# A tuned attention + two-MoE kernel: the constants tile moved by 192 bytes in SBUF

## The reference, cut to what matters

```
x1  = x + attention(rmsnorm(x, norm1_scale), Wq, bq, ..., Wo, bo)      # 16 heads of 16, chunks of 64
...
# first MoE: xf = rmsnorm(x1); top 2 of 8 experts, capacity 1280 rows each
h   = gelu(xf[tok] @ W1[eid] + b1[eid]) @ W2[eid] + b2[eid]            # 256 -> 1024 -> 256
out = out.at[tok].add(gate[:, None] * h)
...
x   = layernorm(x + x1 + out)
# second MoE: xn = layernorm(x) * gamma + beta; top 2 of 8, capacity 1280
g, u = split(xb @ w12.T);  h = silu(g) * u;  yb = h @ w3.T             # 256 -> 2 x 1024 -> 256
x   = layernorm(x + out2)
```

## Time and profile before

| | us |
|---|---|
| median of three executions | 1483.54 |
| lowest of them | 1483.48 |
| profiled execution, its own time | 1478.57 |
| its span, first to last instruction | 1476.8 |

### The profile page before, as it was taken

How to read it: one execution, slowest core, us unless ns; L and a number is a source line. 1 busy time by engine, 2 the same in 40 slices (tenths; PEclk the granted TensorE clock), 3 DMA queues, 4 the chain that set the end, 5 groups by cost and what they waited for, 6 DMA issues and landing times. The chain is left out here.

```text
span 1476.8 us, 36143 instructions
## 1 busy us (share of the span) xinstructions
PE 1410.1 (95%) x11723; PEld 1367.4 (93%) x11723; DVE 1008.9 (68%) x2854; ACT 720.5 (49%) x1791; POOL 776.8 (53%) x792
## 2 busy tenths in 40 slices
PE   8999994899999999999966999999999999999998
PEld 7888883899999999999956999999999999999998
DVE  6999986577677667777674556565565656656686
ACT  5677664455555445555543434434343434444353
POOL 4677651566666666665432444344444334443467
PEclk9999995899999999999966999999999999999999
DMA  8121223343343442443432142322323131321342
GB/s 269 44 72 49 65 69 80 94 108 53 94 101 49 105 102 43 105 127 55 119 132 110 29 117 34 115 36 45 99 35 118 32 114 29 103 51 32 104 148 94
DMA packets 63560, 124.79 MB, mean 85 GB/s; under 512 B 14336, under 2 KB 51840, under 8 KB 60416
## 3 DMA queue, kind: packets, MB, share of 16 engines
q0 software_dynamic: 35936, 47.89, 18.9%
q1 hardware_dynamic: 27552, 76.02, 14.2%
HBM read 80.97 MB, written 42.90 MB: 84 GB/s over the span
## 5 line engine op out<-in xcount | busy, mean ns | idle before, releaser
L1032 POOL DMA_INDIRECT E_mg<-meta,IDX x160 | 151.5, 947 | 313.3 <-DVE E_gate L1254 286.0
L1327 DVE TENSOR_TENSOR E_hraw<-E_sg,bank 128x256 f32<-128x256 f32 x320 | 133.8, 419 | 243.6 <-ACT E_sg L1192 178.0
L1039 POOL DMA_INDIRECT acc<-ysb,IDX x150 | 243.2, 1622 | 82.7 <-issue 45.0
L1397 PE MATMUL bank<-E_xT,ws 128*128 128x256 f32 x960 | 268.6, 280 | 6.2 <-DVE E_xT L1245 5.0
L1398 PE MATMUL bank<-E_xT,ws 128*128 128x256 f32 x960 | 267.3, 278 | 0.0
L1399 PE MATMUL bank<-E_xT,ws 128*128 128x256 f32 x960 | 267.2, 278 | 0.0
L1338 DVE TENSOR_TENSOR E_hT<-E_hraw,E_hT 128x256 fp32r<-128x256 f32 x640 | 259.5, 415 | 0.0
L1334 DVE CAST E_hT<-E_hraw 128x256 fp32r<-128x256 f32 x640 | 202.1, 316 | 66.4 <-ACT E_hraw L1195 61.8
L1192 ACT ACTIVATE E_sg<-bank 128x256 f32<-128x256 f32 x320 | 118.8, 383 | 239.2 <-PE bank L1399 221.7
L1397 PEld LDWEIGHTS bank<-E_xT,ws 128*128 128x128 f32 x960 | 182.5, 190 | 8.3 <-issue 5.8
L1398 PEld LDWEIGHTS bank<-E_xT,ws 128*128 128x128 f32 x960 | 182.6, 190 | 0.0
(11 more groups left out here) (229 smaller groups left out, 3910.8 us busy)
## 6 DMA issues: line engine op xcount, KB each, us to landing
wraw<-in_w_ffn SPq DMA_DIRECT2D x8, 3072.0 KB, 11.2
wraw<-in_w_moe SPq DMA_DIRECT2D x8, 2048.0 KB, 12.7
acc<-x SPq DMA_DIRECT2D x32, 128.0 KB, 1.7
xn<-xn SPq DMA_DIRECT2D x32, 128.0 KB, 1.7
acc<-X POOLq DMA_DIRECT2D x4, 1024.0 KB, 8.4
acc<-X SPq DMA_DIRECT2D x8, 512.0 KB, 4.4
X<-acc SPq DMA_DIRECT2D x7, 512.0 KB, 5.4
X<-in_x SPq DMA_DIRECT2D x3, 1024.0 KB, 11.5
```

The costliest lines, as they stand in the source:

```text
L1032: nc.gpsimd.indirect_dma_start(out=mg[:, j, :], out_offset=None, in_=meta_dram, in_offset=at_slots(u, j)).then_inc(s_gm, 16)
L1039: nc.gpsimd.indirect_dma_start(out=acc_dram, out_offset=at_slots(u, j), in_=ysb[:, j, :], in_offset=None, compute_op=ALU.add).then_inc(s_y ...
L1327: V.tensor_tensor(hraw[:, f % RING, :], sg[:, f % RING, :], bank[f % RING][:, UW:2 * UW], ALU.mult).then_inc(s_hm, 1)
L1397: nc.tensor.matmul(out, wh, mh, start=first, stop=False)
```

## The change

Two tensors that only take room are allocated, one of 48 floats (192 bytes) ahead of the constants and one of 16 floats (64 bytes) behind them. The constants begin 192 bytes later, all that is allocated after them 256 bytes later. Instructions, their order on every engine and their waits are the same as before.

```
--- before.py
+++ after.py
@@ -1630,7 +1630,9 @@
         META = sb("META2", [P, NT, 6])
         LG = sb("LG", [P, NT, E])
         IDX = sb("IDX", [P, SC], I32)
+        sb("pad_c", [P, 48])
         cst = sb("cst", [P, C_N])
+        sb("pad_d", [P, 16])
         small = {"rbias": sb("rbias", [P, E]), "sc_moe": sb("sc_moe", [P, 2 * KD]), "sc_ffn": sb("sc_ffn", [P, 2 * KD]),
                  "wr2": sb("wr2", [P, KD, E])}
         wraw = sb("wraw", [P, 4 * 1536])
```

## The result

In twenty executions each the changed kernel took 1495.74 us (median) and the kernel before 1490.29. The ratio is **1.0043, with a 95% interval of 1.0028 to 1.0058**: within 2%, but a loss clear of noise, and outside the range of 1477 to 1489 us. The ratio compares fast executions alone (it leaves out 1506.20 and 2536.96 us before and 1513.37 after, each over 1.5% above the fastest of its kernel); the quotient of the two medians is 1.0037. The profiled execution took 1494.04 us with a span of 1492.2. Of the 12.2 us between the forecast and the measured median, 6.8 belong to it and 5.4 to the change.

What follows compares the result with a forecast made beforehand. The prediction took TensorE, busy 95% of the span, to bound the kernel. All four edits summed to 0, so it forecast the median of the three runs shown, 1483.5 us, with a range of 1477 to 1489 us.

Steps and rivals of the forecast that it cites:

- What bounds the kernel: TensorE's matmuls, busy 95% of the span; a nanosecond occupying TensorE is one of the kernel, counted between starts.
- the unit's sum of 16.78 us: Second expert phase: 144 matmuls at 113.3 ns plus 0.44 us of transposes give 16.76, against 16.78 us between units.
- edit 1: Identity as moving operand of 582 transposes and small matmuls, moved from 0 to 192 modulo 256: taken as 0.
- Both ends, -6.4 and +2.3 us: Bounds on moving the identity: 582 transposes each gaining 11 ns or losing 4 ns.
- a bound of 1.6: 0.02 us a unit over 80 units: 1.6 us in the whole kernel for all effects of transposes on neighbours.
- The end of -6.4 us: Gain if the 22 ns between spare matmuls' and projections' steps were all address: 11 ns per transpose; rival's chance 0.06.
- The rule on the two read ports: Moving operand and weight load read SBUF independently, so no choice of addresses between them could matter: sum 0.
- The identity takes over the step of the other moving operands: Rival: transposes at 192 lose 4 ns each, +2.3 us, 1485.8 us; chance of a small loss 0.05.
- The shift by 256 bytes: Rivals in the 9600 expert matmuls: a collision opens, 1513 us, or 4 ns each goes, 1445 us; chance 0.02 each.
- edit 3: Rest of SBUF (xT, hT, second expert weight set) moved by 256 bytes, place modulo 256 kept: 0.
- Edits 2 and 4: Constants as operands of VectorE, ScalarE and GpSimd: 0, at most 1.2 us either way; loading the constants at the start: 0.

Runs made afterwards that it cites:

- e6_moving_at_0: The kernel before with the experts' moving operands (xT and the second weights) at 0 modulo 256 instead of 192: ratio 1.0399.
- e2_shift_only: The kernel before with a 256-byte pad behind the constants, so the identity stays and only what is allocated later moves: ratio 0.9997.
- e8_copy_at_192: The kernel before with a second identity copy at 192 modulo 256, read by the expert phases' transposes alone; constants stay at 0, the rest moves 512 bytes: ratio 1.0057.
- e13_identity_224: The kernel before with the identity at 224 modulo 256 and the rest moved by 256 bytes: ratio 1.0013.
- e9_kick_in_mid_unit: The changed kernel with one spare 8-column matmul in the middle of each unit's first product: ratio 1.0140 against the kernel before.

## Why the prediction was wrong

- **What bounds the kernel** was right: the steps of TensorE, and that what counts is the distance of starts. So was the unit's sum of 16.78 us. (The 99.42 of 100 us that it gives for the first expert phase is the next stretch, 400 to 500 us; the earlier trace rows has 99.56.)
- **The step that failed is edit 1**, with the sentence it rests on, that "what the identity's placement could still hide in the matmuls round a transpose is therefore 0.02 us a unit". The closed sum of one unit told what the transposes cost where they stood at 0. It was used as a bound on what they could cost elsewhere. Both ends, -6.4 and +2.3 us, priced the 582 transposes alone, and these did not move: 0.44 us for four, before and after. The cost came in the 142 matmuls behind them, 0.62 us in one unit of four, 8.8 us in the profile by the count, against a bound of 1.6; the ratio of the twenty executions is 6.4 us.
- **The view was at hand.** The chain of waits before had one such unit, and the prediction read only the two rows that suited:

```profile
1042.45 0.52 PE bank L1390 x4
1059.94 0.44 PE bank L1390 x4
```

  They are 17.49 us apart. In order of time, TensorE is held up for a moment at the 30th and 31st matmul behind the transposes (steps of 140 and 221 ns; by what isn't shown) and steps by 0.12 instead of 0.11 us from there on:

```profile
1046.11 0.28 PE L1399 MATMUL bank<-ws,E_hT 128*128 128x256 f32 x1
1046.24 0.38 PE L1397 MATMUL bank<-ws,E_hT 128*128 128x256 f32 x1
1046.47 0.28 PE L1398 MATMUL bank<-ws,E_hT 128*128 128x256 f32 x1
```

  Until 1059.78, when the next transposes come, 115 of the 142 steps are slow. Two steps for one and the same instruction, with an interruption between, were in the trace before the change.
- **The end of -6.4 us** had nothing under it. The steps of 0.243 us for the spare matmuls and 0.222 for the projections came from taking the mean duration of the group off the merged length, where the last matmul's own, 0.398 and 0.401, belongs. From start to start the same trace has 324 and 235 ns for the three spare matmuls and 236 and 231 ns for the three projections, so no 22 ns that could be put down to the address. That 0 is the worse place for a moving operand is true of the expert matmuls, 120 against 113 ns (`e6_moving_at_0`), whose weights stand at 0. The identity's own step is the same at either place, and the trains behind it do worse with it at 192 and the rows at 0.
- **The rule on the two read ports** (the Trainium skill, TensorE: Matmul & The Clock Gate, Part 2) was taken to mean that no choice of addresses could matter. The runs decide against that reading of it: places alone make 4% in `e6_moving_at_0`.
- **The rivals.** "The identity takes over the step of the other moving operands", +2.3 us, had the sign by luck and not the mechanism: a transpose's step is what it was. The shift by 256 bytes does nothing (`e2_shift_only`), as edit 3 said.
- **Edits 2 and 4** held: the row tile's activations have medians of 392 and 388 ns in the two routings instead of 388 and 388, and `e8_copy_at_192` has the whole loss without moving the constants.
- **The range** rested on three executions, two of them 0.06 us apart. The same kernel took 1490.29 in the median of twenty, above the range by itself, and 1471 to 1490 us on other occasions. Of a wander of 5 us the range took only a part, and medians on record lie 19 us apart.

What stays open: what inside TensorE or SBUF makes two trains of identical instructions step by 113 or 118 ns. The runs show that the step depends on places modulo 256 and on how the train begins, and that it is kept for up to 142 matmuls. That the reads of the two operands get in each other's way is a guess, and nothing here looks inside. Open too is why the states that units hand down come round after four units at 192, two at 128, two at 64 (in the second phase with a slow unit among them, in the first without), and one at 0 and 224. No version beats the kernel before; `e13_identity_224` equals it.

## What to carry to other kernels

Read the step of a dense train of matmuls from start to start, unit by unit, and not from mean durations: a kernel at 95% busy hid 4% steps there. An operand's address can cost through the instructions behind it, so a bound from the moved instruction's own time is none. Where to put an operand has to be measured: the identity cost nothing with its rows at an equal place (both at 0 or both at 192) and at 224 with rows at 0, while the expert matmuls were slowest with both operands at 0 and fastest with the moving one at 192. And look in the trace for units that differ from their neighbours before you call a cost fixed.

## What the runs showed of the hardware

- Matmuls of 128x256 in fp32r, weights at 0 modulo 256, step by 120 ns with the moving operand at 0, by 115 to 122 at 128 and 160, by 113 or 118 at 192, and by 115 to 123 at 224, all at a full granted clock.
- At 192 a train keeps either step for up to 142 matmuls. One 8-column matmul in mid train turned 113.3 into 117.8 ns in 36 units of 39 (`e9_kick_in_mid_unit`), and itself cost 0.115 us.
- The beginning of a train is handed down by the one ahead: with the identity at 192 the step into the transposes takes 115, 118 or 119, 121 and 118 ns ahead of units with 4, 142, 1 and 1 slow steps, in rounds of four units; before the change it is 115 ns ahead of 30 of the 33 units of the second phase with 4.
- A transpose of 128x128 in fp32 steps by 109 ns with the identity at 0 and at 192 alike.
